# A second source of hand-fetched rows in the edge stage: ScalarE fetches two table rows per step, GpSimd gathers six chunks fewer

## What is computed

```
x = x + gnn(layernorm(x))      # gnn: z = h W (4 heads x 64); e = leaky_relu(es[src] + ed[dst])
                               # softmax of e over the edges of each dst
                               # out[dst] = sum over its edges of alpha * z[src]
x = x + ffn(layernorm(x))      # top-2 of 16 experts per node, w1, relu, w2, layernorm
```

## Time and profile before

| | |
|---|---|
| median of three runs | 2674.49 us |
| the profiled execution | 2682.39 us, of which span 2680.6 us |
| edge stage, first to last gather issued | 80.4 to 2096.0 us |
| GpSimd busy over the span | 1818.0 us, 68% |
| PE busy over the span | 1841.6 us, 69% |
| VectorE busy over the span | 1771.6 us, 66% |
| ScalarE busy over the span | 782.3 us, 29% |

### The profile page before, as it was taken

The page is one execution under the profiler, slowest core; times in us unless marked ns, Lnnn a source line. Parts: engine busy times, 40 slices in busy tenths (PEclk is TensorE's granted clock), DMA queues, the critical chain, the costliest instruction groups (busy, mean ns, idle before and its releaser), DMA issues. The chain is left out here.

```text
span 2680.6 us, 57054 instructions
## 1 busy us (share of the span) xinstructions
PE 1841.6 (69%) x9027; PEld 1426.8 (53%) x9028; DVE 1771.6 (66%) x5364; ACT 782.3 (29%) x3126; POOL 1818.0 (68%) x1941
## 2 busy tenths in 40 slices
PE   7467556666666666666666656666666459999997
PEld 5345445454544454444444444544544239999985
DVE  6577777777676777767777767777777774333326
ACT  4433112212121221122121112211222225555557
POOL 0677777777777777777777777777777245555547
PEclk9786887877787878888878888887788769999999
DMA  9454445545545555455445555554555127533338
GB/s 320 141 136 134 135 135 144 140 133 139 144 133 138 140 139 136 135 141 139 136 139 137 140 138 136 144 136 133 140 141 136 43 67 245 167 106 105 105 95 283
DMA packets 186614, 380.05 MB, mean 142 GB/s; under 512 B 40054, under 2 KB 90657, under 8 KB 185931
## 3 DMA queue, kind: packets, MB, share of 16 engines
q0 software_dynamic: 87264, 241.69, 33.1%
q1 hardware_dynamic: 76152, 114.56, 13.8%
q10 hardware_dynamic: 22898, 20.85, 3.0%
HBM read 341.68 MB, written 33.93 MB: 140 GB/s over the span
## 5 line engine op out<-in xcount | busy, mean ns | idle before, releaser
L734 POOL DMA_INDIRECT ring<-z_table,src_idx x1602 | 1524.0, 951 | 498.0 <-issue 476.8
L999 PE MATMUL psMb<-msg,S 128*128 128x260 f32 x3608 | 1183.9, 485 | 544.4 <-DVE msg L871 543.8
L999 PEld LDWEIGHTS psMb<-msg,S 128*128 128x128 f32 x3608 | 810.2, 236 | 727.0 <-DVE msg L871 586.4
L871 DVE TENSOR_TENSOR msg<-ring,psPb 128x1024 f32<-128x1024 f32 x451 | 546.7, 1212 | 0.0
L919 ACT COPY es_edge<-ring 128x16 f32 x451 | 91.5, 203 | 1390.2 <-SPq L662 1351.8
L805 DVE TENSOR_TENSOR earg<-es_edge,dest_sum 128x16 f32<-128x16 f32 x451 | 80.3, 178 | 410.0 <-ACT es_edge L919 383.3
L793 DVE TENSOR_TENSOR S<-iota_f,psPb 128x512 f32<-128x512 f32 x451 | 306.6, 680 | 1.8 <-ACT psPb L928 1.8
L988 PEld LDWEIGHTS psEb<-node_thirds,ST 128*128 128x128 bf16 x1804 | 104.1, 105 | 319.1 <-issue 297.2
L787 DVE TENSOR_SCALAR ST<-dst_bc,iota_p 128x512 bf16 x451 | 171.2, 380 | 127.4 <-issue 120.3
L988 PE MATMUL psEb<-node_thirds,ST 128*128 x1804 | 120.9, 179 | 180.5 <-DVE earg L822 94.9
L1264 POOL DMA_INDIRECT rows_sb<-norm_rows,src_sb x108 | 110.3, 1021 | 167.2 <-DVE src_sb L1341 149.4
(11 more groups left out here) (210 smaller groups left out, 1568.4 us busy)
## 6 DMA issues: line engine op xcount, KB each, us to landing
dst_bc<-dst_rows SPq DMA_DIRECT2D x202, 256.0 KB, 3.5
ring<-z_table,src_idx POOLq DMA_INDIRECT x1602
side<-z_table SPq DMA_DIRECT2D x1280, 1.0 KB
w_all<-in_L_ffn_w_dram SPq DMA_DIRECT2D x32, 512.0 KB, 5.9
b_sb<-in_L_ffn_b_dram ACTq DMA_DIRECT2D x108, 128.0 KB, 3.2
got<-pair_rows SPq DMA_DIRECT2D x48, 256.0 KB, 4.2
z_table<-z_out SPq DMA_DIRECT2D x49, 130.0 KB, 6.4
norm_rows<-xnb ACTq DMA_DIRECT2D x49, 128.0 KB, 2.9
```

The costliest lines, as they stand in the source:

```text
L734: nc.gpsimd.indirect_dma_start(ring[:, s, c, :], None, z_table, bass.IndirectOffsetOnAxis(ap=at, axis=0)).then_inc(b_landed[s], 16)
L871: nc.vector.tensor_tensor(msg[:, s % MR, :, 0:D].rearrange("p g (h d) -> p g h d", h=HEADS), ring[:, bass.ds(slot, 1), :, 0:D].rearrange(" ...
L999: last = nc.tensor.matmul(psM[s % 2][:, 0:ROW], S[:, s % MR, c, :], msg[:, s % MR, c, :], start=c == 0, stop=c == G - 1)
```

## The change

ScalarE fetches rows as well. A new stage `bring(i)` stands last in each of its steps: it takes ACT_ROWS = 2 rows, for each an index load from `src_idx` into a register and a one-row DMA into a new buffer `second_side`. 64 steps make a chunk. Six groups (66, 130, 194, 258, 322 and 386 by the formula, moved by one where SyncE already has the group) lose a chunk from GpSimd's list; steps 0 to 383 bring rows. SyncE gets `move_second`, which copies the finished chunk from `second_side` into `ring` two groups ahead, and its relay of such a group waits for that copy as well. GpSimd gathers 1596 chunks.

To make room in SBUF, `resets` moves from the buffers of the first two stages into those of the routing stage (its two memsets with it), and the 512-wide `iota_f` is split into a 128-wide one that is kept and a 512-wide `iota_w` of the first stage, with one more copy on VectorE.

```
+ACT_ROWS = 2
...
-        iota_f = sb(attention, "iota_f", [P, 512])
+        iota_f = sb(attention, "iota_f", [P, P])
...
-        resets = sb(attention, "resets", [P, EXPERTS, NT])
...
-                nc.gpsimd.memset(resets[:, :, :], 1.0).then_inc(a_filled, 1)
...
-                step(nc.vector.tensor_copy(iota_f[:, :], iota_i[:, :]))
+                step(nc.vector.tensor_copy(iota_w[:, :], iota_i[:, :]))
+                step(nc.vector.tensor_copy(iota_f[:, :], iota_i[:, 0:P]))
...
+        ACT_STEPS = P // ACT_ROWS
+        ACT_GROUPS = [g for g in range(ACT_STEPS + 2, GROUPS - RING, ACT_STEPS)]
+        for m, g in enumerate(ACT_GROUPS):
+            ACT_GROUPS[m] = g + (g in BY_HAND)
+        BY_ACT = {g: m for m, g in enumerate(ACT_GROUPS)}
...
-                        return sum(G - (h in BY_HAND) for h in range(s, upto, RING))
+                        return sum(G - (h in BY_HAND) - (h in BY_ACT) for h in range(s, upto, RING))
...
+                        if g in BY_ACT:
+                            sp.wait_ge(b_moved, 16 * (BY_ACT[g] + 1))
...
+                    def move_second(g, m):
+
+                        sp.wait_ge(b_brought[m % 2], 16 * P * (m // 2 + 1))
+                        done = sp.value_load(group_free[0:1, g:g + 1], min_val=0, max_val=VISITS)
+                        sp.wait_ge(b_msg, done + 1)
+                        sp.dma_start(ring[:, g % RING, G - 1, :], second_side[:, m % 2, :]).then_inc(b_moved, 16)
...
+                        if g + 2 in BY_ACT:
+                            move_second(g + 2, BY_ACT[g + 2])
...
-                        for c in range(G - 1 if g in BY_HAND else G):
+                        for c in range(G - 1 if g in BY_HAND or g in BY_ACT else G):
...
+                    def bring(i):
+
+                        m, at = divmod(i, ACT_STEPS)
+                        if m >= len(ACT_GROUPS):
+                            return
+                        if at == 0 and m >= 2:
+                            act.wait_ge(b_moved, 16 * (m - 1))
+                        chunk = ACT_GROUPS[m] * G + G - 1
+                        for p in range(at * ACT_ROWS, (at + 1) * ACT_ROWS):
+                            row = act.value_load(src_idx[p:p + 1, chunk:chunk + 1]).with_bounds(min_val=0, max_val=NT * P - 1)
+                            act.dma_start(second_side[p:p + 1, m % 2, :], z_table[bass.ds(row, 1), :]).then_inc(b_brought[m % 2], 16)
-                    written_out(VISITS, SR, [(open_group, AHEAD + 2), (locate, AHEAD + 3), (exponent, AHEAD + 3), (finish, None)], steps=FINISH)
+                    written_out(VISITS, SR, [(open_group, AHEAD + 2), (locate, AHEAD + 3), (exponent, AHEAD + 3), (finish, None), (bring, None)], steps=FINISH)
...
+                nc.gpsimd.memset(resets[:, :, :], 1.0).then_inc(c_reset, 1)
+                pool.wait_ge(c_reset, 1)
+                nc.gpsimd.memset(resets[:, :, 0:1], 0.0).then_inc(c_reset, 1)
...
+                dve.wait_ge(c_reset, 2)
```

More of the change, by code:

```diff
@@ L251, in gnn_moe_kernel @@
             iota_pi = sb(ctx, "iota_pi", [P, 1], I32)
+            iota_w = sb(ctx, "iota_w", [P, 512])
             below = sb(ctx, "below", [P, 3, 512])
@@ L365, in _ @@
                 nc.gpsimd.memset(valid[:, :], 1.0).then_inc(a_filled, 1)
-                nc.gpsimd.memset(resets[:, :, :], 1.0).then_inc(a_filled, 1)
-                pool.wait_ge(a_filled, 2)
+                pool.wait_ge(a_filled, 1)
                 nc.gpsimd.affine_select(out=valid[:, NT - 1:NT], in_=valid[:, NT - 1:NT], compare_op=ALU.is_ge, fill=0.0,
                                         base=REST - 1, pattern=[[0, 1]], channel_multiplier=-1).then_inc(a_masks, 1)
-                nc.gpsimd.memset(resets[:, :, 0:1], 0.0).then_inc(a_masks, 1)
                 pool.wait_ge(a_const, 5)
@@ L395, in _ @@
                 nc.gpsimd.tensor_copy(dst_col[:, :], dst_i[:, :])
-                pool.wait_ge(a_masks, 4)
+                pool.wait_ge(a_masks, 3)
                 for i in range(2):
@@ L492, in aside @@
                         step(nc.vector.tensor_tensor(thr[:, 4:5], thr[:, 2:3], thr[:, 3:4], ALU.is_gt))
-                        nc.vector.tensor_scalar(below[:, 0, 0:VISITS], iota_f[:, 0:VISITS], thr[:, 2:3], None, ALU.is_ge).then_inc(a_ge, 1)
-                        nc.vector.tensor_scalar(below[:, 1, 0:GROUPS], iota_f[:, 0:GROUPS], thr[:, 1:2], None, ALU.is_gt).then_inc(a_ge, 1)
+                        nc.vector.tensor_scalar(below[:, 0, 0:VISITS], iota_w[:, 0:VISITS], thr[:, 2:3], None, ALU.is_ge).then_inc(a_ge, 1)
+                        nc.vector.tensor_scalar(below[:, 1, 0:GROUPS], iota_w[:, 0:GROUPS], thr[:, 1:2], None, ALU.is_gt).then_inc(a_ge, 1)
                     if t == TABLES + 6:
@@ L500, in aside @@
                         step(nc.vector.scalar_tensor_tensor(out=visit_group[:, :], in0=psA[1][0:1, 0:VISITS], scalar=-1.0,
-                                                            in1=iota_f[0:1, 0:VISITS], op0=ALU.mult, op1=ALU.add))
+                                                            in1=iota_w[0:1, 0:VISITS], op0=ALU.mult, op1=ALU.add))
                         step(nc.vector.tensor_scalar(visit_slot[:, :], visit_group[:, :], RING - 1, None, ALU.bitwise_and))
@@ L509, in aside @@
                         step(nc.vector.tensor_tensor(group_free[:, RING - 1:GROUPS + 1], psA[2][0:1, 0:GROUPS - RING + 2],
-                                                     iota_f[0:1, 0:GROUPS - RING + 2], ALU.add))
+                                                     iota_w[0:1, 0:GROUPS - RING + 2], ALU.add))
                     if t == EARLY + 5:
@@ L572, in gnn_moe_kernel @@
         b_side = [sem(f"b_side{i}") for i in range(2)]; b_placed = sem("b_placed")
+        b_brought = [sem(f"b_brought{i}") for i in range(2)]; b_moved = sem("b_moved")
         b_dst = [sem(f"b_dst{i}") for i in range(PAIRED)]; b_rows = sem("b_rows")
@@ L601, in gnn_moe_kernel @@
         SH = 2 * HEADS
-        PER_PASS = (b_pstep, b_nodes, b_group, *b_side, b_placed, *b_dst, b_rows, b_S, b_ST, b_dest, b_estep, b_arg, b_p, b_msg, b_sum, b_acc, b_es, b_fstep, b_reset, b_rden,
+        PER_PASS = (b_pstep, b_nodes, b_group, *b_side, b_placed, *b_brought, b_moved, *b_dst, b_rows, b_S, b_ST, b_dest, b_estep, b_arg, b_p, b_msg, b_sum, b_acc, b_es, b_fstep, b_reset, b_rden,
                     b_scaled, b_added, b_stats, b_var, b_root, b_ready, b_xn, b_xT_ps, b_xT, b_log_ps, b_log, *b_saved)
@@ L612, in gnn_moe_kernel @@
         BY_HAND = {g: m for m, g in enumerate(HAND_GROUPS)}
+        ACT_STEPS = P // ACT_ROWS
[3 more added lines that the diff above has]
+        BY_ACT = {g: m for m, g in enumerate(ACT_GROUPS)}
+        assert not set(BY_ACT) & set(BY_HAND)
         THIRDS = 3
@@ L633, in gnn_moe_kernel @@
             side = sb(ctx, "side", [P, 2, ROW])
+            second_side = sb(ctx, "second_side", [P, 2, ROW])
             psE = [ps(ctx, f"psEb{i}") for i in range(SR // BANKED)]
@@ L711, in _ @@
                     sp.wait_ge(b_placed, 16 * len(HAND_GROUPS))
+                    for i in range(2):
+                        sp.wait_ge(b_brought[i], 16 * P * len(range(i, len(ACT_GROUPS), 2)))
+                    sp.wait_ge(b_moved, 16 * len(ACT_GROUPS))
                     for done, total in ((b_group, GROUPS), (b_rows, PAIRS), (b_S, VISITS), (b_ST, VISITS), (b_dest, VISITS), (b_estep, 4 * VISITS),
@@ L1025, in gnn_moe_kernel @@
         graph.close()
-        c_vstep = sem("c_vstep"); c_gap = sem("c_gap")
+        c_vstep = sem("c_vstep"); c_reset = sem("c_reset"); c_gap = sem("c_gap")
         c_exp = sem("c_exp"); c_taken = sem("c_taken"); c_rank = sem("c_rank")
@@ L1038, in gnn_moe_kernel @@
             gap = sb(ctx, "gap", [P, 2, NT])
+            resets = sb(ctx, "resets", [P, EXPERTS, NT])
             total = sb(ctx, "total", [P, EXPERTS, NT])
```

## The result

The changed kernel takes 2698.80 us (median of four runs, 2696.94 to 2703.07) against 2675.47 us (median of four, the three of before and one more). The ratio, estimated from all of these runs, is 1.0091 with a 95% interval of 1.0079 to 1.0104. By the medians it is 23 us slower; the forecast was 2677.3, 2.8 us slower, and its range ended at 2686.5.

The account below looks back on a forecast made before the run. GpSimd's list of gathers was taken as the bound. Saving 7.5 us, losing 6.3 at the start and 4.0 at weighing steps gave +2.8 us, 2677.3 us on the median; range 2667.5 to 2686.5.

Parts of the forecast that it names:

- The bound: Edge stage is as long as GpSimd's list of gathers; six fewer at 1.25 us save 7.5 us.
- The price of a pair: Two row fetches in a ScalarE step take 1.97 us of its sequencer, priced from SyncE's rows; lower end 1.5 us.
- rival 2: ScalarE's and SyncE's sequencers hinder each other at issuing; a pair costs 2.5 us, sum +13, 2687.5 us; chance 0.20.
- No running ahead at 84.4: At the edge stage's start, ScalarE's sequencer can't bring rows while its ACTIVATE waits for VectorE, until 84.41 us.
- The start: Eight pairs before visit 1's `es_edge` make it 9.7 us later; GpSimd loses 6.3 us once, at group 4.
- The weighing steps: Where ScalarE waits for VectorE's accumulate, a pair behind it delays `es_edge`; 7 places by 0.6 us or so, loss 4 us.
- the chain of rows 11: ScalarE released at 749.93, `es_edge` at 752.65 after a pair, some 0.75 us late for VectorE; GpSimd's start at 756.24 moves.
- SyncE's `move_second`: Six chunk copies of 0.50 us on SyncE, ahead of relays and its row fetches; costed at 0, bound 1 us.
- The signs to watch: Prediction wrong if GpSimd's first gap, at group 4, is under 2 or over 9 us, or later gaps total over 10.

Follow-up runs that it names:

- both edits: Changed kernel with rows brought only from ScalarE's step 8 on, and before `finish` in each step; 2669.2 us, 0.9978 of before.
- the kernel without fetching: Changed kernel with the six chunks left out of GpSimd's list and neither `bring` nor `move_second`; 2667.7 us, 0.9971 of before.

## Why the prediction was wrong, step by step

- **The bound** was right: GpSimd's list. Cutting it alone gave 7.8 us against 7.5.
- **The price of a pair**, 1.97 us from SyncE's rows, was too low: a step at the start took 2.34 us and not 2.07 (the pair and 0.1 us of handing over). The bounds I named for a pair were 1.5 and, for rival 2, 2.5, so this was inside them; the reason of rival 2 (two sequencers at one descriptor block) was not it. The rule of the Trainium skill behind it, Perfetto Trace Analysis, DMA Instruction (HWDGE), would have made issues shorter without SyncE's rows; they stayed at 0.467 us.
- **No running ahead at 84.4** was right. The first row's DMA stands at 85.14, behind the released ACTIVATE. The rule of the Trainium skill, Advanced Engine Details and Errata, Sequencer Loop, by which it could have come earlier, isn't borne out for ScalarE here.
- **The start**, 6.3 us, has the right mechanism and too small a size: the gap is 8.9 us, and removing it gave 7.3 us. The `es_edge` of visit 1 came 12.6 us later instead of 9.7. Of these 2.9 us, 8 x 0.27 = 2.2 are the dearer pairs and 0.3 the later release (84.67 instead of 84.41).
- **The weighing steps**, 4 us, are the term that failed: taking the rows out of them, or putting the rows ahead of the wait, gave back 20 to 22 us. The place and the mechanism were right, the chain of rows 11 happened as written. Two things were wrong. One `es_edge` was late by more than I reckoned, since from the release it took 3.2 to 3.9 us (3.64 in the example) and not 1.97 + 0.75 = 2.72; the pair is dearer, and the register load behind it slower. And I counted 7 independent places with 0.6 us each, by the share of groups in which a message came last in the trace of before. Where the weighing steps stand was in the code: in triples, every second step. The delays of a triple can add up on VectorE, and GpSimd was stopped at all 13 triples, 1.6 us each on average. A share of coincidences from a trace in which nothing was late says nothing about how many will be late together.
- **SyncE's `move_second`**, costed at 0 with 1 us as the bound, stands for a kernel that has slack: with both edits the whole is within 1.5 us of the kernel without fetching. In the changed kernel it isn't hidden. The relays behind the copy were late, and that is part of the 3.07 us of the example; a gap of 1.7 us at 436 us, behind the copy for group 66 and outside the weighing steps, is another place (1.4 us with the rows before `finish`, 0.7 with both edits, none in the kernel that fetches nothing). How much it cost in all no run separates.
- **The signs to watch** were the right ones: a first gap under 2 or over 9 us, or later gaps of over 10. The first gap, 8.9, stayed just inside; the later gaps, 26.9, did not.

## What to carry to other kernels

Before an idle engine is given work, don't divide its idle time by its steps: find the steps in which others wait for its next result, and how close together they stand. Work put ahead of a wait that is there anyway was free here, the same work behind it went on the path; that order alone was 22 of the 23 us. When a trace of before prices a pattern with delays that it doesn't contain, count the places from the schedule in the code rather than from how often something was the last to come.

## What the runs showed of the hardware

- A one-row DMA costs its issuing sequencer differently by engine and by what stands ahead of it. On SyncE it is 0.26 us behind a register load. On ScalarE it is 0.47 us behind one, with the register's address or a fixed one, and 0.23 to 0.24 right behind another issue.
- On ScalarE the register load of `open_group` takes 0.28 us in the kernel before, 0.48 behind a load and issue of a row, and 0.56 behind two issues in a row. Load and issue in turn have a period of 1.15 us, against 0.99 on SyncE.
- A register load that reads partitions 64 to 127, coming after one that read partition 0, takes 0.46 us, and 0.29 in partitions 0 to 63.
- ScalarE's sequencer did not go on to the next register load while the ACTIVATE ahead of it waited for VectorE: the first row's issue is at 85.14, behind the release at 84.67.
- Six DMAs of a chunk and 768 of a row beside the gathers left the gather's usual step at 1.25 us. The loss wasn't bandwidth: the same rows in another order cost 22 us less.
